# A grouped feed-forward with its routing ahead, shared blocks between routed ones, and one read pass

## The reference, cut to what matters

```
x      = layernorm(x)                              # 1024 tokens x 256
scores = softmax(x @ gate_w.T)                     # 16 experts
topk_w, topk_idx = top_k(scores, 4)
topk_w = topk_w / sum(topk_w)
y  = sum over the 4 chosen experts e of  topk_w[e] * mlp(x, w_gate[e], w_up[e], w_down[e])   # width 176
y += mlp(x, sw_gate, sw_up, sw_down)               # shared, width 352
mlp(x, wg, wu, wd) = silu(x @ wg.T) * (x @ wu.T) @ wd.T
x  = residual + y
```

## Time and profile before

| | us |
|---|---|
| median of 3 executions | 1501.32 (1501.03 to 1511.45) |
| the profiled execution | 1505.28 |
| its span, first to last instruction | 1503.4 |
| first feed-forward: first logits to last scatter's start | 396.6 to 582.2 |
| second feed-forward: the same | 1294.5 to 1478.6 |

### The profile page before, as it was taken

How to read it: one execution, slowest core, us unless ns; L and a number is a source line. 1 busy time by engine, 2 the same in 40 slices (tenths; PEclk the granted TensorE clock), 3 DMA queues, 4 the chain that set the end, 5 groups by cost and what they waited for, 6 DMA issues and landing times.

```text
span 1503.4 us, 28392 instructions
## 1 busy us (share of the span) xinstructions
PE 1312.6 (87%) x8194; PEld 1101.2 (73%) x8194; DVE 1045.4 (70%) x2274; ACT 847.9 (56%) x2102; POOL 870.6 (58%) x764
## 2 busy tenths in 40 slices
PE   5999999999988983749998989899999999978982
PEld 3888888888877883538777767677777778867872
DVE  5666666646777544438888878688888886777544
ACT  1444444454435542238778777677878875436541
POOL 3555555540346774247878777678778650356772
PEclk9999999999979997769999999999999999979996
DMA  3000000001326336221222221122222202326335
GB/s 112 26 26 26 27 25 25 16 9 55 122 84 204 109 103 213 52 58 29 59 59 63 55 68 43 43 61 63 57 69 56 57 1 77 121 92 196 103 103 178
DMA packets 58253, 110.60 MB, mean 74 GB/s; under 512 B 11456, under 2 KB 29440, under 8 KB 57856
## 3 DMA queue, kind: packets, MB, share of 16 engines
q1 hardware_dynamic: 46976, 82.11, 19.3%
q0 software_dynamic: 9024, 24.65, 5.4%
q10 hardware_dynamic: 2112, 2.10, 0.4%
HBM read 63.99 MB, written 15.47 MB: 53 GB/s over the span
## 4 chain that ended last, share of the span: by engine, by line
PE 45%; issue 19%; POOL 17%; DVE 11%; DMA 3%; ACT 2%; SPq 0%; POOLq 0%; DVEq 0%; ACTq 0%
PE ps L1450 31%; PE ps L1596 7%; POOL pb_odd L1089 4%; POOL yt L1089 3%; POOL rb L1074 2%; PE ps L1813 2%; POOL z L1089 2%; PE ps L1538 2%; POOL pb_low L1089 2%; POOL ra L1078 2%; DVE x_res L840 1%; PE ps L1673 1%; DVE pt_lo L902 1%; PE ps L1701 1%; DVE rb L541 1%
## 5 line engine op out<-in xcount | busy, mean ns | idle before, releaser
L902 DVE TENSOR_TENSOR pt_lo<-ps,pt_hi 128x512 fp32r<-128x512 f32 (+3 forms) x384 | 205.6, 548 | 54.8 <-ACT pt_hi L1369 48.4
L1450 PE MATMUL ps<-kh,qh 128*128 128x512 f32 (+3 forms) x768 | 204.1, 376 | 22.3 <-DMA qh<-qt_hi 10.2
L887 DVE TENSOR_REDUCE nmb<-ps 128x1 f32<-128x1024 f32 (+7 forms) x256 | 191.8, 749 | 29.1 <-PE ps L1450 28.1
L1369 ACT CAST pt_hi<-ps 128x512 fp32r<-128x512 f32 (+3 forms) x384 | 178.5, 481 | 58.7 <-PE ps L1813 53.1
L1450 PEld LDWEIGHTS ps<-kh,qh 128*128 128x128 f32 x768 | 132.3, 196 | 46.2 <-issue 14.3
L1450 PE MATMUL ps<-pt_hi,vst 128*128 128x512 f32 (+3 forms) x384 | 157.0, 409 | 0.9 <-DVE ra L867 0.8
L1450 PE MATMUL ps<-pt_lo,vst 128*128 128x512 f32 (+3 forms) x384 | 132.9, 350 | 0.0
L994 POOL TENSOR_TENSOR pa<-pa,rinv 128x384 f32<-128x384 f32 x64 | 52.9, 827 | 134.5 <-DVE rinv L581 134.5
L1167 ACT ACTIVATE pa<-ps,nmax 128x192 f32<-128x192 f32 x128 | 53.1, 423 | 131.0 <-DVE nmax L575 131.0
L1029 POOL DMA_INDIRECT xg<-zbuf,gidx x94 | 97.6, 1039 | 41.3 <-issue 23.8
L1089 POOL TENSOR_TENSOR pb_odd<-pb_odd,rib 128x1024 f32<-128x1024 f32 (+1 forms) x64 | 105.3, 1670 | 21.9 <-DVE rib L894 21.3
(11 more groups left out here) (222 smaller groups left out, 4219.9 us busy)
## 6 DMA issues: line engine op xcount, KB each, us to landing
raw_w<-in_wx SPq DMA_DIRECT2D x36, 608.0 KB
rb<-raw SPq DMA_DIRECT2D x192, 64.0 KB, 2.0
yg<-ybuf SPq DMA_DIRECT2D x16, 512.0 KB, 4.9
qh<-qt_hi SPq DMA_DIRECT2D x64, 128.0 KB, 2.3
qh<-qt_lo SPq DMA_DIRECT2D x64, 128.0 KB, 2.4
wa<-in_wa SPq DMA_DIRECT2D x16, 384.0 KB, 3.0
wb<-in_wb SPq DMA_DIRECT2D x8, 384.0 KB, 3.4
wo_a<-in_wo_a SPq DMA_DIRECT2D x16, 128.0 KB, 2.0
```

The costliest lines, as they stand in the source:

```text
L887: v.tensor_reduce(nmb[:, par, i:i + 1], ps[:, b:b + 2, :].rearrange("p b k -> p (b k)")[:, 0:P * (t + 1)], AX.X, ALU.max, negate=True).the ...
L902: v.tensor_tensor(pt_lo[:, s % 3, at], ps[:, 4 + s % 2, at], pt_hi[:, s % 3, at].bitcast(F32), ALU.subtract).then_inc(sem("b_pt_lo"), 1)
L1369: s_.copy(pt_hi[:, s % 3, at], ps[:, 4 + s % 2, at]).then_inc(sem("b_pt_hi"), 1)
L1450: return t_.matmul(o, l, r, start=start, stop=stop)
```

## The change

The change has five parts. (1) The layernorm of the first half, its logits and its choice move into the output projection's last steps. The numbers of the experts that the choice compares with become an input of their own (`ie`), so that it need not wait for the constants. (2) The rest of the routing is moved together: `starts` and `places` behind step 3, `hot` behind 4 and 5, `tables` behind step 6; on TensorE the second logits stay at step 4, `ranks` go to step 5, `table` to 7 and 8. The gather's row numbers are made ahead of the scatter's. (3) The order of the blocks is: 12 shared, r0, r1, two shared, r2, r3, two shared, r4 to r46. (4) GpSimd makes the low parts of weights 0 to 7 only, and the tables that give the steps of the weight copies are new. (5) In `ybuf` the four outputs of a token lie in consecutive rows, so that a partition reads 4 KB at a time; four DMAs of two tiles each bring all of it into a buffer that holds all 8 tiles. The low part of the value weights of the next attention (first feed-forward alone) goes ahead of the sums.

```
+FRONT = 12
+ORDER = ([("s", n) for n in range(FRONT)] + [("r", 0), ("r", 1), ("s", 12), ("s", 13), ("r", 2), ("r", 3), ("s", 14), ("s", 15)] +
+         [("r", b) for b in range(4, NB)])
+AT = {item: j for j, item in enumerate(ORDER)}
-POOL_LO = 9
+POOL_LO = 8
-YG_RING = 4
+TILE_ROWS = TOPK * P + TOPK
...
-                yg = sb("yg", [P, YG_RING, TOPK, D], c=over)
+                yg = sb("yg", [P, NT, TOPK * D], c=over)
...
                 sp.dma_start(wg[:, :, :], d["wg"]).then_inc(sem(f"{s}_consts"), 16)
+                sp.dma_start(ie[:, :], d["ie"]).then_inc(sem(f"{s}_consts"), 16)
                 load(1)
...
-                for t in range(NT):
-                    if t >= YG_RING:
-                        sp.wait_ge(sem(f"{s}_added"), since(s, "added") + t - YG_RING + 1)
-                    first = P * (1 + TOPK * t)
-                    sp.dma_start(yg[:, t % YG_RING, :, :],
-                                 ybuf[first:first + TOPK * P, :].rearrange("(k p) e -> p k e", p=P)).then_inc(
-                        sem(f"{s}_yl{t % YG_RING}"), 16)
+                tiles = ybuf[0:NT * TILE_ROWS, :].rearrange("(t r) e -> t r e", r=TILE_ROWS)
+                for n in range(NT // 2):
+                    sp.dma_start(yg[:, 2 * n:2 * n + 2, :],
+                                 tiles[2 * n:2 * n + 2, 0:TOPK * P, :].rearrange("t (p k) e -> p t (k e)", k=TOPK)).then_inc(
+                        sem(f"{s}_yl{n}"), 16)
@@ VectorE, the output projection's second half, behind out_lo(s, 1, h) @@
-                    elif h == 12:
+                    elif h == 10:
                         norm_lo(nxt, 0, 0)
+                    elif h == 14:
+                        picked(nxt, 0)
@@ VectorE, tables() @@
-                    link(v.scalar_tensor_tensor(out=row[:, :], in0=tb[:, 1, :], scalar=float(P), in1=tb[:, 0, :],
+                    link(v.tensor_scalar(pick[:, :], tb[:, 1, :], 1.0, -1.0, ALU.max, ALU.add))
+                    link(v.tensor_scalar(tile[:, :], pick[:, :], 2, None, ALU.arith_shift_right))
+                    ins = v.scalar_tensor_tensor(out=gidx[:, :], in0=tile[:, :], scalar=float(P), in1=tb[:, 0, :],
+                                                 op0=ALU.mult, op1=ALU.add)
+                    ins.then_inc(sem(f"{s}_idx"), 1)
+                    dve.wait_ge(sem(f"{s}_idx"), since(s, "idx") + 1)
+                    link(v.scalar_tensor_tensor(out=row[:, :], in0=gidx[:, :], scalar=float(TOPK), in1=pick[:, :],
                                                 op0=ALU.mult, op1=ALU.add))
-                    v.tensor_tensor(sidx[:, :], row[:, :], dump[:, :], ALU.add)
-                    link(v.tensor_scalar(tile[:, :], pick[:, :], 2, None, ALU.arith_shift_right))
-                    v.scalar_tensor_tensor(out=gidx[:, :], in0=tile[:, :], scalar=float(P), in1=tb[:, 0, :],
-                                           op0=ALU.mult, op1=ALU.add).then_inc(sem(f"{s}_idx"), 1)
+                    v.tensor_tensor(sidx[:, :], row[:, :], dump[:, :], ALU.add).then_inc(sem(f"{s}_idx"), 1)
@@ VectorE, ffn @@
-                v.memset(hb[:, :, :], 0.0)
+                v.memset(hb[:, :, I_E:P + 64], 0.0)
+                v.memset(hb[:, :, I_E + 64:2 * P], 0.0)
                 residual(before, 1)
                 mean_square(s, before, 1)
                 variance(s, 1)
                 mul(0)
                 step(0)
                 normalized(s, 1)
-                picked(0)
                 step(1)
                 norm_lo(s, 1, ACC[before][1])
                 step(2)
+                picked(s, 1)
                 step(3)
-                picked(1)
+                starts()
+                places()
+                step(4)
+                hot(0)
+                step(5)
+                hot(1)
+                step(6)
+                experts()
+                tables()
                 shifted()
-                step(4)
-                step(5)
-                starts()
-                step(6)
-                places()
-                step(7)
-                hot(0)
-                step(8)
-                hot(1)
-                experts()
-                step(9)
-                step(10)
-                tables()
-                for j in range(11, NM):
+                for j in range(7, NM):
                     step(j)
@@ GpSimd, scatter @@
+                    pool.wait_ge(sem(f"{s}_idx"), since(s, "idx") + 2)
@@ ScalarE, the output projection's second half @@
-                    elif h == 11:
+                    elif h == 9:
                         norm(nxt, 0, 0)
                         keep_z(nxt, 0)
@@ TensorE, the output projection's second half @@
-                    if h == 10:
+                    if h == 7:
                         norm(nxt, 0, 0)
+                    elif h == 11:
+                        logits(nxt, 0)
@@ TensorE, ffn @@
-                logits(0)
                 gate_up(0)
                 for j in range(NM):
                     if j == 2:
                         norm(s, 1, ACC[before][1])
                     elif j == 4:
-                        logits(1)
-                    elif j == 6:
+                        logits(s, 1)
+                    elif j == 5:
                         ranks()
-                    elif j == 9:
+                    elif j == 7:
                         table(0)
-                    elif j == 10:
+                    elif j == 8:
                         table(1)
-                    if j + 2 >= NSH and j + 2 < NM:
-                        turn_x(j + 2 - NSH)
+                    if j + 2 < NM and ORDER[j + 2][0] == "r":
+                        turn_x(ORDER[j + 2][1])
...
-ACT_HI = {0: (2,), 2: (3,), 4: (4,), 5: (5,), 7: (6,), 8: (7,), 10: (8,), 11: (9,), 13: (10,), 14: (11,),
-          16: (12,), 18: (13,), 20: (14,), 22: (15,), 24: (16,), 26: (17,)}
-DVE_LO = {12: (9,), 14: (10,), 15: (11,), 17: (12,), 19: (13,), 21: (14,), 23: (15,), 25: (16,), 27: (17,)}
+ACT_HI = {0: (2,), 2: (3,), 4: (4,), 6: (5,), 8: (6,), 9: (7,), 12: (8,), 14: (9,), 16: (10,), 17: (11,),
+          19: (12,), 20: (13,), 22: (14,), 23: (15,), 25: (16,), 26: (17,)}
+DVE_LO = {13: (8,), 15: (9,), 17: (10,), 18: (11,), 20: (12,), 21: (13,), 23: (14,), 24: (15,), 26: (16,), 27: (17,)}
```

More of the change, by code:

```diff
@@ L100, in build @@
             topf = sb("topf", [P, NT, 8], c=own)
+            ie = sb("ie", [P, NE], c=own)
             ex = sb("ex", [P, NT, TOPK], c=own)
@@ L620, in out_lo, with link_, picked @@
                                 ALU.subtract).then_inc(sem(f"{s}_ot_lo"), 1)
+            linked = {"f": 0, "g": 0}
+            def link_(s, ins):
+                linked[s] += 1
+                ins.then_inc(sem(f"{s}_route"), 1)
+                dve.wait_ge(sem(f"{s}_route"), since(s, "route") + linked[s])
+            def picked(s, half):
+                four = slice(4 * half, 4 * half + 4)
+                picks = slice(4 * half * TOPK, (4 * half + 4) * TOPK)
+                dve.wait_ge(sem(f"{s}_logits"), since(s, "logits") + half + 1)
+                link_(s, v.tensor_copy(lg[:, four, :],
+                                   ps[:, 3, 64 * half:64 * half + 64].rearrange("p (t e) -> p t e", e=NE)))
+                for t in range(4 * half, 4 * half + 4):
+                    ins = v.max(top[:, t, :], lg[:, t, :])
+                link_(s, ins)
+                for t in range(4 * half, 4 * half + 4):
+                    ins = v.max_index(topi[:, t, :], top[:, t, :], lg[:, t, :])
+                link_(s, ins)
+                link_(s, v.tensor_copy(topf[:, four, :], topi[:, four, :]))
+                dve.wait_ge(sem(f"{s}_consts"), since(s, "consts") + 32)
+                link_(s, v.tensor_tensor(hit[:, picks, :].rearrange("p (t k) e -> p t k e", t=4),
+                                     ie[:, :].unsqueeze(1).unsqueeze(1).broadcast_to([P, 4, TOPK, NE]),
+                                     topf[:, four, 0:TOPK].unsqueeze(3).broadcast_to([P, 4, TOPK, NE]),
+                                     ALU.is_equal))
+                with nc.allow_low_precision(reason="a sum of 0s and 1s, at most 4"):
+                    v.tensor_reduce(chosen[:, four, :], hit[:, picks, :].rearrange("p (t k) e -> p t e k", t=4),
+                                    AX.X, ALU.add).then_inc(sem(f"{s}_chosen"), 1)
             def out_proj(s, nxt):
@@ L1584, in _, with logits @@
             all_pairs(pe, head_a)
+            def logits(s, half):
+                pe.wait_ge(sem(f"{s}_xt_lo"), since(s, "xt_lo") + 2 * half + 2)
+                if half == 0:
+                    pe.wait_ge(sem(f"{s}_wg_lo"), since(s, "wg_lo") + 1)
+                for t in range(4 * half, 4 * half + 4):
+                    last = three(ps[:, 3, NE * t:NE * t + NE], lambda c, a: xt(a, c, P * t, P),
+                                 lambda c, b: (wg_hi, wg_lo)[b][:, c, :])
+                last.then_inc(sem(f"{s}_logits"), 1)
             def out_proj(s, nxt):
@@ L1608, in out_proj @@
                     step(1, h)
```

(16 more changed lines are left out.)

126 lines of the change are left out of this document (50 added, 76 removed).

## The result

The changed kernel takes **1528.30 us** (median of 4 runs, 1526.55 to 1531.64) where the kernel before takes 1503.09 beside it: ratio 1.0164, 95% interval 1.0137 to 1.0190. The forecast was 1512.1 with a range to 1523: slower than any value in it. The profiled execution has a span of 1524.7 us against 1503.4, so there are 21.3 us to explain.

The account below looks back on a forecast made before the run. It took GpSimd's unbroken indirect transfers from r8's gather, itself waiting for TensorE's r4 transposes, to set the stage's end. 6.3 + 5.3 + 1.4 - 0.7 - 1.5 = +10.8 us gave 1512.1 on the median; range 1491 to 1523.

Parts of the forecast that it names:

- Rivals B and C: B: weights 6, 7 cast before the tables, 1493 us, chance 0.20; C: tables end 3 us later, 1518, chance 0.08.
- One sign that the prediction had named as being against it: Feed-forward, routed half: the prediction is wrong if GpSimd is not without gaps after r8's gather.
- r8's gather: GpSimd's gather for routed block 8, waiting for r4's transposes: forecast +6.3 us in the first stage, +5.3 in the second.
- Weight casts: Behind r8's gather: seven VectorE low parts instead of five lengthen gathers, 0.36 us each, 0.7 a stage, +1.4 in all.
- eight steps from r0 to r4: TensorE's four shared and four routed steps between r0's and r4's rows: 18 us, between 15.9 and 22.2.
- rival A: Those eight steps take 22.2 us instead of 18, +4.2 in each stage: 1520.5 us, chance 0.22.
- the second of A's two reasons: In the eight steps, TensorE comes out of 9 us without work; where it had stalls, its mean clock was 0.78.
- the end of the stage is r8's gather plus 114.7: Routed half: GpSimd runs without longer gaps, so its last scatter follows that gather by 114.7 us (113.1 in the second stage).
- The read pass: Sums at each stage's end: one DMA brings two tiles, -0.7 us in the first stage and -1.5 in the second.
- the 5.4 us of the prediction's rows and the 4.4 of its estimate: Time of a 1 MB read before the sums: 5.4 us by profile rows, kept; 4.4 by the skill's fit, total 2 lower.

Follow-up runs that it names:

- e1: Kernel after, with all 16 shared blocks ahead of r0 again: 1510.6 us, ratio 1.0048 to the kernel before.
- e2: Kernel after, with ScalarE's copies of weights 4 to 7 in steps 3 to 6 instead of 4, 6, 8 and 9: 1514.0 us.
- e8: Kernel after with 16 shared blocks first and VectorE's 128x960 low-part cast of late weights in four pieces of 128x240: 1509.8 us.
- e13: Kernel after with a third place for raw weights alone (weights 8, 11, 14, 17 land in the rows z): 1520.5 us.
- e4: Kernel after with early weight copies, r0 to r5 behind 12 shared blocks, weights 16 and 17 one step later: 1514.6 us.
- e5: Kernel before with the one read pass alone (four reads of 1 MB, scatter rows made behind gather indices): 1509.9 us, ratio 1.0043.
- e11: Kernel before with the one read pass and a third place for raw weights: 1500.2 us, ratio 0.9989.
- e6: Kernel after with 16 shared blocks first; ScalarE copies raw late weights in place of VectorE's 128x960 subtraction (low parts wrong): 1511.9 us.

## Why the prediction was wrong

*Right:* the place and the order of events. Second choice 415.16 (414.1 said), indices 440.93 (441.7), ScalarE's copies of weights 6 and 7 behind the tables and GpSimd's casts back to back, first gather 450.84 (451.1), TensorE idle 9.90 us (9). e1 and e2 show both halves of that mechanism by undoing them. The first gate-up starts at 400.40, 1.2 us later than said, and the indices are on time all the same. Rivals B and C did not happen. One sign that the prediction had named as being against it did: GpSimd is not without gaps behind r8's gather (1.12 us at 479.36).

*The step that failed: "Weight casts", +1.4, measured +7.7.* It priced the denser casts by the longer gathers beside them, 0.36 us each for two more, and took GpSimd to run without gaps. The transfers themselves grew by 2.1 us a stage, three times the price, and waits make up the rest. e8 removes the length, and the stretch of its profile is no shorter; e13 removes the wait for raw weights and gets 2.5 and 2.4 of the 2.9 and 4.8 us back. The prediction followed the moved casts on VectorE and GpSimd and did not follow them to the load that SP may only issue when a cast is done. A load takes 3.7 to 4.8 us on the chain of the kernel after, a cast 1.6; with two places and casts a step and a half apart, ScalarE has to wait. The first sign was in the trace of before: its own 1.14 us wait for weight 2, used there for one step and not asked of the rest. A longer one stands among the very steps up to r4 (ScalarE, kernel before):

```profile
459.29 1.21 ACT L1249 CAST w_ex<-raw_w 128x1216 fp32r<-128x1216 f32 x1 [1.62 <-DMA raw_w<-in_wx]
```

What is left in the second stage (115.5 against 113.1) stays open.

*A mis-sized term: eight steps from r0 to r4,* taken as 18 us, 19.9 and 19.5 measured, just below the 20 from which rival A was to decide. e2, where TensorE comes to r0's rows without a stop and has the same casts in these steps, has 17.9 and 17.6. So the missing 1.9 goes with the second of A's two reasons, TensorE's long stop and the clock of 0.50 behind it, and not with the casts; the third place leaves these steps at 19.7 (e13). With this term r8's gather is explained in the first stage (8.1 for 6.3). In the second it was 3.2 us later than said: some 1.5 by these steps, and 1.5 because the first gather comes 1.0 us later than in the kernel before and not 0.5 earlier, for which no run gives a reason.

*Also off:* "the end of the stage is r8's gather plus 114.7" held for the kernel before and not as a rule (e4: 130.1). The read pass was sized about right (-1.0 and -1.9 for -0.7 and -1.5); alone, without the moved cast, it is worth less, and a late weight then cost more than it gave (e5, e11).

## What to carry to other kernels

When work is moved along an in-order list, follow each operation backwards to the load it needs and to the event that frees that load's place: a ring of two that was hardly ever late turns into the bound when its users come closer together. A stretch in which one engine has no gaps is not yet bound by it alone; ask which engine goes along at the same pace, since a shorter list on the first only shows the second. Making a result earlier is worth what its consumer can do with it: here the indices came 10 us sooner, and the fill that was moved behind the gathered rows left TensorE idle.

## What the runs showed of the hardware

*Indirect transfers beside a cast.* In the timelines of the kernel after, VectorE's cast of two operands in SBUF ends at 494.61 + 0.42 = 495.03, and the gather that began within it ends at 494.06 + 1.39 = 495.45, 0.42 later (the other transfers beside a cast: 0.38 to 0.43); a gather on its own lasts 0.97. Counted from the end of the first of the two instructions, the one in hand when the gather began (493.44 + 1.15 = 494.59), it is 0.86, and 0.81 to 0.86 for the others.

```profile
493.44 1.15 DVE L759 TENSOR_TENSOR w_ex<-raw_w,w_ex 128x960 fp32r<-128x960 f32 x1
494.61 0.42 DVE L760 TENSOR_TENSOR w_ex<-raw_w,w_ex 48x256 fp32r<-48x256 f32 x1
```

In four pieces the same cast leaves gathers of 1.03 and scatters of 1.10 to 1.15 (e8); a transfer that begins within the 48x256 instruction alone ends 0.82 to 0.89 behind it there and in e6. By these rows the transfer waits for the instruction in hand and not for the next one. The Trainium skill (SBUF — State Buffer, "Who interferes with whom") says that a VectorE instruction with two SBUF inputs holds off GpSimd instructions that read SBUF until it ends, and infers that descriptor generation is not among them; the rows agree on the waiting. An indirect transfer reads its row numbers from SBUF, too; whether that reading is what waits, or the descriptors after all, no run here separates.

*Reads issued together.* The 1 MB reads, four issued together in each stage, land 4.9 (least), 8.1 (median) and 11.3 us (most) after their issue in the kernel after; the least lies between the 5.4 us of the prediction's rows and the 4.4 of its estimate. So the first sums start later than with 512 KB reads (600.85 - 593.14 = 7.7 us behind the last scatter, 6.6 before) and then run on without a wait.
